# A DMA ring of four instead of three for the state projection's weights, and the down-projection's scale moved into the weight dequantisation

## The reference

```python
state = jnp.tanh(jnp.einsum('bsd,nd->bsn', x, B))        # B: 1024 x 2048
attn  = jnp.einsum('bsn,dn->bsd', state, C) + D * x      # C: 2048 x 1024
def _qlinear(x, wq, scale):
    W = (wq.astype(jnp.float32) - ZERO_POINT) * scale[:, None]
    return jnp.einsum('bsd,hd->bsh', x, W)
ffn   = _qlinear(silu(_qlinear(x, wq_gate, s_gate)) * _qlinear(x, wq_up, s_up), wq_down, s_down)
x = x + attn(_layernorm(x));  x = x + ffn(_layernorm(x)) # hidden 5632, rows 8 * 4096
```

## Time and profile before

| | us |
|---|---|
| median of 2 runs | 5657.34 (5656.89 to 5657.8) |
| profiled execution | 5665.09 |
| its span, core 0, the slowest | 5663.5 |
| its spans on the 8 cores | 5632.9 to 5663.5 |
| mean granted TensorE clock, core 0 | 0.941 |

### The profile page before, as it was taken

One profiled execution on the slowest core, in us unless ns is written; L12 is line 12 of the kernel. 1 busy time (PEld: TensorE's weight loads), 2 busy tenths in 40 slices (PEclk: granted clock), 3 DMA queues, 4 the chain that ended last, 5 costly groups with the idle time before them and its releaser, 6 DMA issues.

```text
span 5663.5 us, 52572 instructions; the slowest of 8 cores (5632.9 to 5663.5 us)
## 1 busy us (share of the span) xinstructions
PE 4321.1 (76%) x20368; PEld 2067.9 (37%) x20736; DVE 917.5 (16%) x1472; ACT 460.2 (8%) x640; POOL 93.9 (2%) x179
## 2 busy tenths in 40 slices
PE   0000048997799959996899879995999789987998
PEld 0000024443444434443444444443444344444444
DVE  2222211111111121111211111112111111111101
ACT  0000011000101011000110011101100010001100
POOL 0111100000000000000000000000000000000000
PEclk9999989998899979997999989997999899988999
DMA  9999954455345454455345534544455534553444
GB/s 309 324 327 330 331 167 140 153 178 185 105 152 172 144 150 147 153 174 171 119 153 176 179 115 152 176 145 148 144 152 173 176 115 153 177 176 109 152 149 160
DMA packets 382911, 992.40 MB, mean 175 GB/s; under 512 B 161360, under 2 KB 161360, under 8 KB 355408
## 3 DMA queue, kind: packets, MB, share of 16 engines
q1 hardware_dynamic: 215136, 794.48, 43.3%
q10 hardware_dynamic: 142336, 100.68, 6.5%
q0 software_dynamic: 25200, 93.86, 4.3%
HBM read 844.19 MB, written 111.15 MB: 169 GB/s over the span
## 4 chain that ended last, share of the span: by engine, by line
PE 70%; DMA 24%; DVE 2%; issue 2%; ACT 2%; ACTq 1%; SPq 0%; DVEq 0%; POOLq 0%
PE PS L599 22%; PE PS L533 21%; PE PS L543 21%; DMA WBB<-sb_img 8%; DMA LQ<-wdi 4%; DMA LQ<-wgi 4%; PE PS L500 3%; DMA LQ<-wui 3%; PE PS L523 2%; ACT TRA L333 1%; DMA WDB<-sd_img 1%; DVE HTM L419 1%; ACTq L341 1%; DMA WCB<-sc_img 1%; DMA HFM<-HTM 1%
## 5 line engine op out<-in xcount | busy, mean ns | idle before, releaser
L533 PE MATMUL PS<-HFM,WGU 128*128 128x512 bf16 (+1 forms) x5784 | 1298.3, 377 | 132.2 <-DMA HFM<-HTM 123.3
L599 PE MATMUL PS<-WDB,GFM 128*128 128x512 bf16 x5520 | 1223.5, 382 | 75.4 <-DMA WDB<-sd_img 69.5
L543 PE MATMUL PS<-HFM,WGU 128*128 128x512 bf16 x5512 | 1261.6, 379 | 6.9 <-DMA WGU<-su_img 0.6
L500 PE MATMUL PS<-HFM,WBB 128*128 128x256 bf16 x2048 | 368.4, 352 | 1080.1 <-DMA HFM<-HTM 755.9
L533 PEld LDWEIGHTS PS<-HFM,WGU 128*128 128x128 bf16 x5888 | 589.8, 100 | 790.0 <-issue 135.7
L599 PEld LDWEIGHTS PS<-WDB,GFM 128*128 128x128 bf16 x5632 | 554.0, 98 | 744.8 <-issue 89.3
L543 PEld LDWEIGHTS PS<-HFM,WGU 128*128 128x128 bf16 x5632 | 551.0, 98 | 663.6 <-issue 1.2
L500 PEld LDWEIGHTS PS<-HFM,WBB 128*128 128x128 bf16 x2048 | 237.9, 122 | 1210.1 <-issue 1137.4
L459 DVE SCALAR_TENSOR_TENSOR GFM<-PS,SUC,GFM 128x512 bf16<-128x512 f32 x352 | 264.5, 751 | 2206.0 <-PE PS L543 2206.0
L347 ACT ACTIVATE GFM<-PS,SGC 128x512 bf16<-128x512 f32 x352 | 241.4, 687 | 2125.0 <-PE PS L533 2124.9
L523 PE MATMUL PS<-WCB,SFM 128*128 128x512 bf16 x992 | 259.5, 403 | 25.5 <-DMA WCB<-sc_img 22.0
(11 more groups left out here) (30 smaller groups left out, 360.9 us busy)
## 6 DMA issues: line engine op xcount, KB each, us to landing
WGU<-sg_img SPq DMA_DIRECT2D x352, 512.0 KB, 3.7
WGU<-su_img SPq DMA_DIRECT2D x352, 512.0 KB, 3.7
WDB<-sd_img SPq DMA_DIRECT2D x321, 512.0 KB, 3.6
WBB<-sb_img SPq DMA_DIRECT2D x256, 256.0 KB, 3.4
LQ<-wgi SPq DMA_DIRECT2D x44, 1024.0 KB, 46.7
LQ<-wui SPq DMA_DIRECT2D x44, 1024.0 KB, 46.8
LQ<-wdi SPq DMA_DIRECT2D x44, 1024.0 KB, 46.3
XT<-xin ACTq DMA_DIRECT2D x32, 1024.0 KB, 8.3
```

Of the source, the lines that this page charges most:

```text
L500: ins = tensor.matmul(PS[:, n, lo:hi], WBB[(2 * u + c // 8) % 3][:, c % 8, :], HFM1[:, c, lo:hi], start=(c == 0), stop=(c == DC - 1))
L533: ins = tensor.matmul(PS[:, 4 + hc % 2, lo:hi], WGU[t % 3][:, c, :], HFM2[:, c, lo:hi], start=(c == 0), stop=(c == DC - 1))
L543: ins = tensor.matmul(PS[:, 6 + hc % 2, lo:hi], WGU[t % 3][:, c, :], HFM2[:, c, lo:hi], start=(c == 0), stop=(c == DC - 1))
L599: ins = tensor.matmul(PS[:, bank, :], GFM[:, hc, g * 128:(g + 1) * 128], WDB[u % 3][:, q * 512:(q + 1) * 512], start=(hc == 0), stop=(hc = ...
```

## The change

- The ring `WBB` gets a fourth buffer and semaphore. Load `h` now waits for unit `(h - 4) // 2`: both loads of unit k need unit k-2 finished. Four instead of three loads are issued ahead, at the end of the pass before.
- The down scale is multiplied into the weights when they are converted: for the 44 down units DVE runs a `scalar_tensor_tensor`, (LQ - 128) * SDP, instead of the one-operand addition. `SDP` holds the scales of one slice of 512 columns, four times over, for 11 units; SP loads it (1 MB) ahead of units 0, 11, 22 and 33. From the second on the load waits until all units before are converted.
- The evacuation of the down product is one addition, `XT` plus PSUM; `TMPD`, `SDB`, its load and DVE's wait for it are gone.

```diff
+                if kind == "D" and i % 11 == 0:
+                    s_ = i // 11
+                    if s_ > 0:
+                        sync.wait_ge(sem["P_DQ"], NU_B + NU_C + NU_G + NU_U + 11 * s_)
+                    sync.dma_start(out=SDP[:], in_=sdq[s_]).then_inc(sem["LSDP"], 16)
@@
-            sync.dma_start(out=SDB[:], in_=sdb).then_inc(sem["LDS"], 16)
@@ def emit_b
-                if h >= 3:
-                    sync.wait_ge(sem["MM_ST"], (h - 3) // 2 + 1)
-                sync.dma_start(out=WBB[h % 3][:],
+                if h >= 4:
+                    sync.wait_ge(sem["MM_ST"], (h - 4) // 2 + 1)
+                sync.dma_start(out=WBB[h % 4][:],
@@
-                            if p > 0 and half == 0 and 2 * n + hh < 3:
+                            if p > 0 and half == 0 and 2 * n + hh < 4:
@@
-                    for q in range(3):
+                    for q in range(4):
                         emit_b(p + 1, 0, q // 2, q % 2)
@@ vector, preparation, down units
+                    vector.wait_ge(sem["LSDP"], 16 * (i // 11 + 1))
+                    vector.scalar_tensor_tensor(WOUT[u % 8][:, :D], LQ[o % 10][:],
+                                                -128.0, SDP[:], ALU.add,
+                                                ALU.mult).then_inc(sem["P_DQ"], 1)
@@
-            vector.wait_ge(sem["LDS"], 16)
@@ vector, end of a pass
-                        if 16 * p + e >= 1:
-                            vector.wait_ge(sem["EV_DN"], 16 * p + e)
-                        ds_inc(vector.tensor_tensor(TMPD[:],
-                                                    PS[:, (s % 2) * 4 + g, :],
-                                                    SDB[:, s * 512:(s + 1) * 512],
-                                                    ALU.mult))
-                        ds_wait()
                         vector.tensor_tensor(XT[xb(p, g)][:, s * 512:(s + 1) * 512],
                                              XT[xb(p, g)][:, s * 512:(s + 1) * 512],
-                                             TMPD[:],
+                                             PS[:, (s % 2) * 4 + g, :],
                                              ALU.add).then_inc(sem["EV_DN"], 1)
@@ tensor
-                                tensor.wait_ge(LWB[h % 3], 16 * (h // 3 + 1))
+                                tensor.wait_ge(LWB[h % 4], 16 * (h // 4 + 1))
```

More of the change, by code:

```diff
@@ L57, in build_nc @@
     suc = nc.dram_tensor("suc", [128, HC], F32, kind="ExternalInput").ap()
-    sdb = nc.dram_tensor("sdb", [128, D], F32, kind="ExternalInput").ap()
+    sdq = nc.dram_tensor("sdq", [SL, 128, D], F32, kind="ExternalInput").ap()
     dcol = nc.dram_tensor("dcol", [128, DC], F32, kind="ExternalInput").ap()
@@ L75, in build_nc @@
         IDENT = E(nc.sbuf_tensor("IDENT", [128, 128], BF16))
-        TMPD = E(nc.sbuf_tensor("TMPD", [128, 512], F32))
         DDIAG = E(nc.sbuf_tensor("DDIAG", [128, DC, 128], BF16))
@@ L93, in build_nc @@
             WOUT = [P_(nc.sbuf_tensor(f"WOUT{i}", [128, 2 * D], BF16)) for i in range(8)]
-        SDB = E(nc.sbuf_tensor("SDB", [128, D], F32))
+            SDP = P_(nc.sbuf_tensor("SDP", [128, D], F32))
         XT = [E(nc.sbuf_tensor(f"XT{b}", [128, D], F32)) for b in range(NXB)]
@@ L102, in build_nc @@
         WGU = [E(nc.sbuf_tensor(f"WGU{i}", [128, DC, 128], BF16)) for i in range(3)]
-        WBB = [E(nc.sbuf_tensor(f"WBB{i}", [128, DC // 2, 128], BF16)) for i in range(3)]
+        WBB = [E(nc.sbuf_tensor(f"WBB{i}", [128, DC // 2, 128], BF16)) for i in range(4)]
         WCB = [E(nc.sbuf_tensor(f"WCB{i}", [128, NCH // 2, T], BF16)) for i in range(4)]
@@ L110, in build_nc @@
         sem = {}
-        for name in ["LDC", "LDS", "P_DQ",
+        for name in ["LDC", "LSDP", "P_DQ",
                      "MM_ST", "MM_AT", "MM_G", "MM_U", "MM_DN", "FR_D",
@@ L120, in build_nc @@
         STX = [E(nc.semaphore(f"STX{i}")) for i in range(NXB)]
-        LWB = [E(nc.semaphore(f"LWB{i}")) for i in range(3)]
+        LWB = [E(nc.semaphore(f"LWB{i}")) for i in range(4)]
         LWC = [E(nc.semaphore(f"LWC{i}")) for i in range(4)]
@@ L183, in emit_b @@
                 h = 2 * u + hh
-                if h >= 3:
-                    sync.wait_ge(sem["MM_ST"], (h - 3) // 2 + 1)
-                sync.dma_start(out=WBB[h % 3][:],
+                if h >= 4:
+                    sync.wait_ge(sem["MM_ST"], (h - 4) // 2 + 1)
+                sync.dma_start(out=WBB[h % 4][:],
                                in_=sb_img[n][:, hh * 8:(hh + 1) * 8, :]
-                               ).then_inc(LWB[h % 3], 16)
+                               ).then_inc(LWB[h % 4], 16)
             def emit_c(p, sp, si, h2_):
@@ L374, in _ @@
                                        BF32[u % 2][:, :w]).then_inc(sem["P_DQ"], 1)
-                else:
+                elif kind in ("G", "U"):
                     o = u - (NU_B + NU_C)
@@ L379, in _ @@
                                              LQ[o % 10][:], -128.0).then_inc(sem["P_DQ"], 1)
+                else:
+                    o = u - (NU_B + NU_C)
+                    vector.wait_ge(PLD2[o % 10], 16 * (o // 10 + 1))
+                    vector.wait_ge(sem["LSDP"], 16 * (i // 11 + 1))
+                    vector.scalar_tensor_tensor(WOUT[u % 8][:, :D], LQ[o % 10][:],
+                                                -128.0, SDP[:], ALU.add,
+                                                ALU.mult).then_inc(sem["P_DQ"], 1)
             for i in range(8):
@@ L498, in _ @@
                                 h = 2 * u + c // 8
-                                tensor.wait_ge(LWB[h % 3], 16 * (h // 3 + 1))
+                                tensor.wait_ge(LWB[h % 4], 16 * (h // 4 + 1))
                             ins = tensor.matmul(PS[:, n, lo:hi],
-                                                WBB[(2 * u + c // 8) % 3][:, c % 8, :],
+                                                WBB[(2 * u + c // 8) % 4][:, c % 8, :],
                                                 HFM1[:, c, lo:hi],
@@ L628 @@
     suc = np.ascontiguousarray(su.reshape(HC, 128).T)
-    sdb = np.ascontiguousarray(np.broadcast_to(sd[None, :], (128, D)))
+    sdq = np.ascontiguousarray(
+        np.broadcast_to(sd.reshape(SL, 1, 1, 512), (SL, 128, 4, 512)).reshape(SL, 128, D))
     dcol = np.ascontiguousarray(Dv.reshape(DC, 128).T)
@@ L645 @@
     common = dict(wgi=wgi, wui=wui, wdi=wdi, bmi=bmi, cmi=cmi, sgc=sgc, suc=suc,
-                  sdb=sdb, dcol=dcol, ident=ident)
+                  sdq=sdq, dcol=dcol, ident=ident)
     in_maps = [dict(xin=np.ascontiguousarray(x[i * TOK:(i + 1) * TOK]), **common)
```

1 line of the change is left out of this document (removed).

## The result

| | before | after |
|---|---|---|
| median, us | 5667.88 (10 runs) | 5512.32 (11 runs) |
| profiled execution's span, core 0, us | 5663.5 | 5516.8 |
| mean granted clock, core 0 | 0.941 | 0.957 |

The ratio after to before is 0.9715, 95% interval 0.970 to 0.973: faster by 2.85%, clear of the 2% line. The ratio leaves executions out in which one half of the chip ran at a lower clock; the medians of this table hold them, so the ratio is the better number (0.9715 x 5657.3 = 5496 us). The forecast was 5518, with a range of 5473 to 5578.

The account below looks back on a forecast made before the run. The prediction saw PE waiting for `WBB` loads in the state projections (692.7 us, half waiting). Terms -136 - 25 + 18.5 + 4.6 - 1 = -139 us took 5665.1 to 5526, less 7.8 to the median: 5518, range 5473 to 5578.

Parts of the forecast that it names:

- passes 1 to 7, each: State projection of the later passes: fewer waits for `WBB` with four buffers, -19.4 us each, -136 us in all.
- pass 0: State projection of the first pass, with no stores and only two `XT` loads: -25 us (19 to 30).
- preparation: Weight conversion before the first matmul: `SDP` bytes +12.8, three queue drains +7.5, `XT` load -2.8; together +18.5 us.
- `WDB` wait: Start of the down product: the fourth `WBB` load puts 0.26 MB in front, 0.65 us seven times, +4.6 us.
- end of the run, behind the last matmul: Last evacuation, now one addition: stores start 0.8 us earlier, -1 us.
- The ladder: Pass 1 state projection, second load then half a unit of matmuls: four buffers load a unit ahead, first long wait stays.
- The signs: What would show it: state projection phases 68 to 71 us, `WBB` waits 100 to 180, `WDB` 74, first matmul near 774.
- The gate: State projection, pass 1: the second half needs group 3's transpose, about 39 us after the first half starts.
- More in flight, each later: Rival, chance 0.14: denser `WBB` loads delay ACT's transfers, `TPS[3]` lands 5 us later; -73 us, 5584.
- Full price of the drains: Rival, chance 0.06: in the preparation each of three queue restarts costs 46.3 us; 5650.
- Depth not missing: Rival, chance 0.03: PE waits for bytes, not early issue, so the state projection keeps its pace; +22 us, 5679.
- Even turns: Rival, chance 0.14: SP's loads share DMA engines evenly with ACT's, only `TPS[3]` gates; -188 us, 5469.

Follow-up runs that it names:

- e1_ring4: The kernel before with only the ring of four `WBB` buffers, scale and preparation untouched; ratio to before 0.9738 (0.9662 to 0.9814).
- e2_scale: The changed kernel with the `WBB` ring back at three, keeping the moved scale and single addition; ratio to before 1.0025 (0.9996 to 1.0053).
- e3_sdp2: The changed kernel with a second `SDP` buffer, so its four loads need not wait for the queue to drain; ratio to before 0.972.
- e10_wide: The changed kernel with `WBB` as two whole-unit buffers, each loaded by one 512 KB DMA; ratio to before 0.9725 (0.959 to 0.9861).

## Why the prediction was right

| term | forecast | core 0 | mean of 8 cores |
|---|---|---|---|
| passes 1 to 7, each | -19.4 | -18.8 | -19.9 |
| pass 0 | -25 | -23.8 | -22.8 |
| preparation | +18.5 | +10.7 | +10.6 |
| `WDB` wait | +4.6 | +13.0 | +2.2 |
| end of the run, behind the last matmul | -1 | -0.9 | -0.9 |
| output stage | 0 | -11.1 | -13.6 |

- **The ladder.** Right in mechanism and size, because each load was given the latency of the row with the same neighbours. The step that one would skip, that the first stall stays, is what kept the forecast from being too large: loads 4 and 5 still took 8.8 and 10.0 us. In pass 1 I had the second half begin 39.1 us behind the first and the phase end at 68.6; it was 38.6 and 66.0. The walk gave unit 3's loads no delay of their own; the second took 15.0 us from issue to landing, and unit 3 ended at 21.2 instead of 18.3. Over the run PE waited 207.8 us for `WBB`, more than the 180 of the forecast, and its own busy time fell by 49 us with the clock: that the sum of both came out right is in part luck.
- **The signs.** Phases of 68 to 71 us: 69.0 on core 0. First half ended by the transpose at about 39: mostly, at 38.4. First matmul near 774: 766.6. `WBB` waits of 100 to 180 us and `WDB` waits of 74: 207.8 and 82.6, both missed.
- **The gate.** `TPS[3]` at 39.1 was forecast, 38.4 measured in pass 1, 37.5 in the mean. But it was not the only end of the first half: it came last in 41 of 56, and the first load of unit 8 landed at 36.6 us in the mean. It became the limit of every half only with six buffers.
- **The preparation.** Mis-sized by the drains: 7.5 forecast, 0.3 to 1.2 measured. I took the pause in reads for lost time and left only part of it to the writes; the DMA rate fell to 165 GB/s for 4 us and rose over its mean afterwards. The bytes (3 of 4 loads at 9.6 to 10.0 us) were right, and the conversion's 2.29 us stayed hidden.
- **The `WDB` wait.** The runs do not resolve the 4.6 us. The mean is +2.2 in after and +0.6 in `e1_ring4`, which have the additional load, and +2.0 in `e2_scale`, which does not; single cores of after lie between -12.7 and +13.0 against before.
- **The missing term.** I priced PE's clock inside the phase and let it end there. The 13.6 us behind it are the largest error of the sum; the drains' 6.3 to 7.2 us and most of the small ones go the same way. The forecast of -139 us stands against -162.5 in the mean span, and 5518 against the ratio's 5496. That it lies only 6 us over the median is chance.
- **The rivals.** More in flight, each later: ACT's chain did lengthen (`TPS[3]` 36.1 to 37.5, and 34.3 to 37.5 where the ring alone changes, `e2_scale` to after) but not by 5 us. Full price of the drains: refuted by `e3_sdp2`. Depth not missing: refuted by `e1_ring4`. Even turns: loads still took 8.8 us, so no, although `e10_wide` is a hint of turns of some kind.

## What to carry to other kernels

When a consumer waits for loads that are issued only as it finishes, walk the ring one load at a time and give each the latency of its actual neighbours in the trace; then ask which other input comes due, here a transpose at the end of a store, load and norm chain. A fold that moves work off an engine with slack (the scale here) bought nothing, and its new loads were paid in full on a saturated stage; a broadcast view gives the same fold for a quarter of the bytes. A moved preload lengthens the wait of whatever stands behind it in the same queue, so price both ends of the queue.

## What the hardware showed that I had not expected

- Three drains of the load queue, one of them seen as 12 us without a unit for DVE, cost 0.3 to 1.2 us together: the DMA rate was 165 GB/s for 4 us, then 354 and 386 against a mean of 328.
- The stage behind a stalled one ran at a higher granted clock once the stalls were shorter: 0.963 in place of 0.910 over all cores and passes, 289.3 us instead of 302.9.
- A 512 KB load with 4 KB rows lands among 8 KB-row transfers earlier than two of 256 KB with 2 KB rows: 13.8 us behind the phase's start instead of 16.7, for the second unit in line. Whether the width, the smaller number of DMAs or the order of start does it is open.
